# Two-direction ConvLSTM recurrences: seven packed 128-row operands in place of nine, and the state's rounding moved to ScalarE

## The reference

```python
def step(carry, xr):
    h, c = carry
    inp = jnp.concatenate([xr, h], axis=1)
    gates = lax.conv_general_dilated(inp, w_mid, (1,), 'SAME', dimension_numbers=dn) + b[None, :, None]
    i, f, g, o = jnp.split(gates, 4, axis=1)
    c2 = jax.nn.sigmoid(f) * c + jax.nn.sigmoid(i) * jnp.tanh(g)
    h2 = jax.nn.sigmoid(o) * jnp.tanh(c2)
    return ((h2, c2), h2)
```

## Time and profile before

| | us |
|---|---|
| median of 3 runs | 2088.05 |
| lowest, highest | 2082.49, 2180.3 |
| the profiled execution | 2081.32 |
| its span | 2079.5 |

### The profile page before, as it was taken

One profiled execution on the slowest core, in us unless ns is written; L12 is line 12 of the kernel. 1 busy time (PEld: TensorE's weight loads), 2 busy tenths in 40 slices (PEclk: granted clock), 3 DMA queues, 4 the chain that ended last, 5 costly groups with the idle time before them and its releaser, 6 DMA issues. The chain is left out here.

```text
span 2079.5 us, 43778 instructions
## 1 busy us (share of the span) xinstructions
PE 1838.4 (88%) x16306; PEld 1197.7 (58%) x16306; DVE 1388.5 (67%) x2550; ACT 1064.7 (51%) x1961; POOL 708.4 (34%) x583
## 2 busy tenths in 40 slices
PE   6979269999999999509999999999835999999999
PEld 5545147777777777207777777777512545555555
DVE  5538968888888888457888888888674234333434
ACT  1116147777777776346777777777561222222320
POOL 2010046666666655225666666665300000000000
PEclk9999679999999999759999999999976999999999
DMA  1769320000000000850000000000193001110100
GB/s 65 258 197 213 98 61 23 23 23 23 23 23 23 24 23 10 136 145 25 23 23 23 23 23 23 24 23 23 21 183 82 18 18 33 33 28 23 33 18 26
DMA packets 74618, 111.10 MB, mean 53 GB/s; under 512 B 11856, under 2 KB 31152, under 8 KB 74512
## 3 DMA queue, kind: packets, MB, share of 16 engines
q1 hardware_dynamic: 74512, 109.50, 20.3%
HBM read 71.71 MB, written 37.75 MB: 53 GB/s over the span
## 5 line engine op out<-in xcount | busy, mean ns | idle before, releaser
L668 PE MATMUL gates_l<-xh_l,w_hi_l 112*112 112x512 f32 x3072 | 819.5, 402 | 117.1 <-DVE keep_l L730 117.1
L668 PEld LDWEIGHTS gates_l<-xh_l,w_hi_l 112*112 112x112 f32 x3072 | 537.7, 175 | 315.4 <-issue 117.8
L644 POOL TENSOR_TENSOR xh_l<-xf_l,xh_l 48x512 fp32r<-48x512 f32 x256 | 360.1, 1407 | 281.8 <-ACT xh_l L687 281.4
L668 PE MATMUL gates_l<-xh_l,w_lo_l 112*112 112x512 f32 x1536 | 450.5, 402 | 0.0
L639 POOL TENSOR_TENSOR xh_l<-hs,xh_l 48x512 fp32r<-48x512 f32 x254 | 303.2, 1194 | 173.8 <-DVE hs L759 173.8
L668 PEld LDWEIGHTS gates_l<-xh_l,w_lo_l 112*112 112x112 f32 x1536 | 270.1, 176 | 97.9
L1174 PE MATMUL b_dw<-b_hid,b_diag 32*32 32x512 f32 x9120 | 313.1, 599 | 0.0
L699 ACT ACTIVATE gate_if_l<-gates_l 112x512 f32<-112x512 f32 x256 | 153.0, 598 | 246.9 <-PE gates_l L668 246.9
L739 DVE TENSOR_TENSOR keep_l<-gate_if_l,cell_l 48x512 f32<-48x512 f32 x256 | 175.5, 685 | 140.8 <-ACT gate_if_l L699 140.8
L1174 PEld LDWEIGHTS b_dw<-b_hid,b_diag 32*32 32x32 f32 x9120 | 185.7, 103 | 116.0 <-issue 48.3
L748 DVE TENSOR_TENSOR cell_l<-keep_l,add_l 48x256 f32<-48x256 f32 x512 | 196.7, 428 | 26.6
(11 more groups left out here) (148 smaller groups left out, 1236.4 us busy)
## 6 DMA issues: line engine op xcount, KB each, us to landing
xf_l<-rows SPq DMA_DIRECT2D x256, 96.0 KB, 2.0
hs<-rows SPq DMA_DIRECT2D x32, 384.0 KB, 10.3
rows<-hs SPq DMA_DIRECT2D x32, 384.0 KB, 5.0
xr<-in_x_rows SPq DMA_DIRECT2D x24, 256.0 KB, 2.7
xc<-in_x_cols SPq DMA_DIRECT2D x24, 256.0 KB, 3.0
mixed<-stage SPq DMA_DIRECT2D x24, 256.0 KB, 3.0
edged<-stage SPq DMA_DIRECT2D x24, 256.0 KB, 3.2
mixed_sb<-mixed SPq DMA_DIRECT2D x32, 192.0 KB, 3.7
```

What stands on the lines that cost most here:

```text
L644: pool.tensor_tensor(xh[far[d]:far[d] + C, d, s, 1, :, 1:W + 1], xf[far[d]:far[d] + C, s, :].rearrange("p (b w) -> p b w", b=B), xh[far[d] ...
L668: mm = nc.tensor.matmul(ps[d][m][0:K, :], weight[:, d, m, t, :], xh[0:K, d, s, part, :, t:t + W], start=(first and t == 0), stop=(last and ...
```

## The change

The same three products are packed in seven matmuls of 128 rows for each pair of gates, 14 in all. Three (one for each tap, weight chunks 1 to 3) take the tile HI of `xh`: the state's rounded part (times w_lo), x's remainder (times w_hi), and in the 32 rows that used to be empty the rounded part of 32 channels of x (times w_lo). Three (chunks 4 to 6) take the tile LO: the state's remainder, a *copy of the state's rounded part* on the other partitions, and the same 32 channels of x, all times w_hi. One (chunk 0) takes the tile `xc`: the last 16 channels of x in three shifts, twice (times w_hi and w_lo), and two rows of ones for the bias.

- SP: the rows that fill the gaps and `xc` come by four transfers from SBUF to SBUF for each step of each direction (`spread`), of 16 x 2 rows, 16 x 2 rows, 48 rows and 48 rows of 2112 bytes. They wait for the gates of the step that last used the slot. The x of both directions is loaded under one semaphore.
- ScalarE rounds x of both directions in one instruction of 112 rows, once for both directions, after the tanh of the cell of direction 1. Between the gates of direction d it rounds the state of the other direction in two halves (`state_hi`) and copies it (`copy_state`). The tanh of g is written back to its own accumulator.
- VectorE writes the unrounded state to `hs` in two halves and nothing else of it. The i x g product stays in the accumulator and the cell is one instruction. `cell` has one PSUM bank for both directions.
- The weights, 128 x 3136, are loaded into rows of `hs` not in use yet and split there by two casts and four masked subtractions.

The core of the diff (indentation reduced, removed lines of the loops left out since they are printed above):

```diff
-w_hi = sb("w_hi", [K, 2, 2, 3, K], F32R)
-w_lo = sb("w_lo", [K, 2, 2, 3, K], F32R)
...
+NCH = 7
+NW = 2 * NCH * 2 * K
+raw = hs[:, H // 2:H // 2 + WROWS, :].rearrange("p a n -> p (a n)")[:, 0:NW]
+w = sb("w", [P, 2, NCH, 2, K], F32R)
+mask = sb("mask", [P, 2, 2])
+xs = sb("xs", [P, 2, FLAT + 2 * LEAD], F32R)
+xh = sb("xh", [P, 2, 2, 2, FLAT], F32R)
+xc = sb("xc", [P, 2, 2, FLAT], F32R)
+gate_o = sb("gate_o", [P, 2, BW])
+keep = sb("keep", [P, BW])
...
+        def spread(d, s):
+            for a in range(2):
+                some = x_rows(s, slice(far[d] + a * GAP, far[d] + (a + 1) * GAP)).bitcast(F32)
+                sp.dma_start(xh[a * HALF + C:(a + 1) * HALF, d, s, :, :].bitcast(F32), some.unsqueeze(1).broadcast_to([GAP, 2, FLAT])
+                             ).then_inc(x_spread[d][s], 16)
+            rest = xs[far[d] + 2 * GAP:far[d] + C, s, LEAD - 1:LEAD - 1 + FLAT].bitcast(F32)
+            shifts = bass.AP(rest.tensor, rest.offset, [list(rest.ap[0]), [1, 3], [1, FLAT]])
+            for c in range(2):
+                sp.dma_start(xc[3 * GAP * c:3 * GAP * (c + 1), d, s, :].bitcast(F32), shifts).then_inc(x_spread[d][s], 16)
...
+        def step(k, more=2):
             for s in range(2):
+                done, ahead, split = (held(sp, 2 * k + (s + n)) for n in (1, 2, 3))
+                row_f, row_b = split, held(sp, k * -2 + (H - 4 - s))
+                if s < more:
+                    sp.wait_ge(x_lo[0], ahead)
+                    sp.wait_ge(x_lo[1], ahead)
+                    load(row_f, row_b, 1 - s)
+                for d in range(2):
+                    sp.wait_ge(gates[d][1], done)
+                    if d == 0:
+                        sp.wait_ge(x_hi, split)
+                    spread(d, s)
...
+                        split_lo(2 * k + (s + 2), d, s)
+                    if not last or s == 0:
+                        state_lo(2 * k + s, 2 * k + s if d == 0 else k * -2 + (H - 1 - s), d, s)
...
+                    def chunk(m, q, tile, lo, first=False, last=False):
+                        return nc.tensor.matmul(ps[d][m][0:K, :], w[:, d, q, m, :], padded(tile)[:, :, lo:lo + W],
+                                                start=first, stop=last)
+                    pe.wait_ge(x_spread[d][s], SPREAD * k + SPREAD)
+                    pe.wait_ge(sig_if[d], 2 * k + (s + 1))
+                    pe.wait_ge(sig_o[d], 2 * k + (s + 1))
+                    pe.wait_ge(cells[d], 2 * k + (s + 1))
+                    for m in range(2):
+                        chunk(m, 0, xc[:, d, s, :], 1, first=True)
+                    pe.wait_ge(x_lo[d], 2 * k + (s + 1))
+                    pe.wait_ge(h_hi[d], 2 * k + (s + 1))
+                    for m in range(2):
                         for t in range(3):
+                            chunk(m, 1 + t, xh[:, d, s, HI, :], t)
+                    pe.wait_ge(h_copy[d], 2 * k + (s + 1))
+                    pe.wait_ge(h_lo[d], 2 * k + (s + 1))
                     for m in range(2):
+                        for t in range(3):
+                            mm = chunk(m, 4 + t, xh[:, d, s, LO, :], t, last=(t == 2))
+                        mm.then_inc(gates[d][m], 1)
...
+        def state_hi(t, row, d, s):
+            n = near[d]
+            for j, part in enumerate(parts):
+                act.wait_ge(h_full[d], t * 2 + (j + 1))
+                hi = nc.scalar.activation(padded(xh[n:n + C, d, s, HI, :])[:, j * HB:(j + 1) * HB, 1:W + 1],
+                                          state(row, d)[:, part].rearrange("p (b w) -> p b w", b=HB), ACT.Copy)
+            hi.then_inc(h_hi[d], 1)
+        def copy_state(row, d, s):
+            f = far[d]
+            nc.scalar.activation(inner(xh[f:f + C, d, s, LO, :]), wide(state(row, d)), ACT.Copy).then_inc(h_copy[d], 1)
...
+                    if d == 0:
+                        earlier, row, slot = 2 * k + (s - 1), k * -2 + (H - s), s
+                        some = not (first and s == 0)
+                    else:
+                        earlier, row, slot = 2 * k + s, 2 * k + s, 1 - s
+                        some = not (last and s == 1)
+                    act.wait_ge(gates[d][0], 2 * k + (s + 1))
+                    nc.scalar.activation(gate_if[0:K, d, :], ps[d][0][0:K, :], ACT.Sigmoid).then_inc(sig_if[d], 1)
+                    if some:
+                        state_hi(earlier, row, 1 - d, slot)
+                    act.wait_ge(gates[d][1], 2 * k + (s + 1))
+                    nc.scalar.activation(ps[d][1][n:n + C, :], ps[d][1][n:n + C, :], ACT.Tanh).then_inc(tanh_g[d], 1)
+                    if some:
+                        copy_state(row, 1 - d, slot)
+                    nc.scalar.activation(gate_o[f:f + C, d, :], ps[d][1][f:f + C, :], ACT.Sigmoid).then_inc(sig_o[d], 1)
+                    act.wait_ge(cells[d], 2 * k + (s + 2))
+                    for j, part in enumerate(parts):
+                        nc.scalar.activation(tanh_c[f:f + C, j, 0:PART], cell[f:f + C, part],
+                                             ACT.Tanh).then_inc(tanhs[d], 1)
+                if s < more:
+                    split_hi(2 * k + (s + 3), 1 - s)
...
+                    dve.wait_ge(sig_if[d], 2 * k + (s + 2))
+                    dve.wait_ge(cells[d], 2 * k + (s + 1))
+                    nc.vector.tensor_tensor(keep[n:n + C, :], gate_if[f:f + C, d, :], cell[f:f + C, :],
+                                            ALU.mult).then_inc(kept[d], 1)
+                    dve.wait_ge(tanh_g[d], 2 * k + (s + 1))
+                    nc.vector.tensor_tensor(ps[d][1][n:n + C, :], gate_if[n:n + C, d, :], ps[d][1][n:n + C, :],
                                             ALU.mult).then_inc(added[d], 1)
+                    dve.wait_ge(kept[d], 2 * k + (s + 1))
+                    dve.wait_ge(added[d], 2 * k + (s + 1))
+                    nc.vector.tensor_tensor(cell[f:f + C, :], keep[n:n + C, :], ps[d][1][n:n + C, :], ALU.add
+                                            ).then_inc(cells[d], 1)
+                    dve.wait_ge(sig_o[d], 2 * k + (s + 2))
                     row = 2 * k + s if d == 0 else k * -2 + (H - 1 - s)
                     whole = hs[n:n + C, bass.ds(row, 1), :].rearrange("p a n -> p (a n)")
+                    for j, part in enumerate(parts):
+                        dve.wait_ge(tanhs[d], 4 * k + (2 * s + j + 1))
+                        nc.vector.tensor_tensor(whole[:, part], gate_o[f:f + C, d, part], tanh_c[f:f + C, j, 0:PART],
+                                                ALU.mult).then_inc(h_full[d], 1)
...
```

275 lines of the change are left out of this document (134 added, 141 removed).

## The result

| | before | after |
|---|---|---|
| median, us | 2085.27 (4 runs) | 2107.57 (4 runs) |
| the profiled execution, us | 2081.32 | 2105.0 |
| its span, us | 2079.5 | 2102.8 |

After to before is 1.0119, 95% interval 1.0092 to 1.0147: slower by 1.2%, within the 2% that I took as the bound and gave a chance of 0.10. One of the four executions before took 2180.3 us, in a slower state of the chip, and the ratio leaves it out. I had forecast 2197 us with a range of 2125 to 2255. The sign was as forecast and the size was not: 24 us in the profiled executions where I had 116.

The account below looks back on a forecast made before the run. TensorE bounds it before, ScalarE after; 127 pairs (a pair: both directions' slots of one time step) x (9.36 - 8.59) = +98, plus 18 for the layers' starts, on 2081.3: 2197 us, range 2125 to 2255.

Parts of the forecast that it names:

- The sign: Whole kernel: slower, chance 0.87; within 2% 0.10, faster 0.03.
- ScalarE takes TensorE's place as the bound: Recurrences: ScalarE's own work is 8.88 us a pair, over today's 8.59, while TensorE falls to 3.35 a slot.
- The order of the chain and the wait for the cell: Each slot: ScalarE's fixed instruction order, in which it waits 0.27 us for VectorE's cell before the tanh.
- Durations: ScalarE's instruction lengths per slot: half rounding about 0.42 us, tanh of g 0.58, summing to 3.93.
- The step that failed: ScalarE's chain in each slot: instruction durations plus handovers of 0.03 us, giving 9.36 a pair with the x rounding.
- My lower bound: Recurrence pair: halves of 0.35 and a tanh of 0.56 take 0.32 us off, to 9.04.
- rival 1: Recurrences: the cell wait hides, ScalarE packed at 8.88 us a pair; 2136 us, 2101 with 0.35 halves; chance 0.12.
- Rival 2: Recurrences: TensorE's clock falls to 1.2 GHz, making it the bound at 11.96 us a pair; 2527 us; chance 0.07.
- Rival 3: Recurrences: TensorE goes on setting the pace at 6.70 us a pair; 1859 us; chance 0.03.
- rival 4: Recurrences: a spread lands late, each microsecond past 13 costing one per pair; 2451 us at 15; chance 0.04.
- TensorE's slack: Recurrences: TensorE idle 1.3 us of each slot, first gates ready 0.5 to 1.1 us before ScalarE wants them.
- Transfers: Recurrences: four more SBUF-to-SBUF transfers per slot, 338 KB, hidden at no cost; DMA engines some 33% busy.

## Why the prediction was right or wrong

- *The sign* is no credit to the sum. Of the forecast's 116 us 98 lay in the pairs, which measured 1.3 less in each layer; that the kernel is slower at all is owed to the starts, and their 26 us had terms of another size and kind than the 18 forecast.
- *ScalarE takes TensorE's place as the bound.* Right: ScalarE 91% busy, two more matmuls a slot cost nothing, one more copy cost 66 us.
- *The order of the chain and the wait for the cell.* Right: forecast 0.27, measured 0.28 to 0.30; VectorE's pieces (0.61, 0.79, 0.73) came within 0.02.
- *Durations.* Nearly right. The group of the half roundings:

```profile
L759 ACT ACTIVATE xh_l<-hs 48x256 fp32r (+1 forms) x504 | 181.5, 407 | 6.1
```

  They are 407 ns where I had 420, and the tanh of g is 569 where I had 580. For the half the Trainium skill, page "VectorE: DVE Perf Modes", section "The TRN2 errata — SBUF-src ops pay a fixed extra latency per instruction", gave an estimate of 0.40; the measurement sides with the page, and that is worth 0.05 of the 0.78 (four halves a pair).
- *The step that failed* is the one that added durations and a handover of 0.03 for each instruction. From start to start the two halves take 0.74 and 0.63, not 0.87; the two tanh 0.55 and 0.64, not 0.72; the rounding of x 0.52, not 0.66. That is 0.76 of 0.78 us a pair, 97 us in 127 pairs. Shorter instructions are 0.07 of it (0.05 the halves); the rest is overlap. With the same chain and the measured pitches the pair is 8.58. My lower bound (halves of 0.35, 9.04 a pair) varied the length of the instructions and never their overlap, so the forecast's own span, from 2146, could not reach the result, and the range was carried down to 2125 only by half of rival 1. The trace of before did have a sign, on VectorE, which I read past: its group of cell halves,

```profile
L748 DVE TENSOR_TENSOR cell_l<-keep_l,add_l 48x256 f32<-48x256 f32 x512 | 196.7, 428 | 26.6
```

  has 428 ns each, yet two in a row took 0.77 and not 0.86.
- *Rival 1*, ScalarE packed at 8.88 (2136 us, or 2101 with halves of 0.35), is nearest in time and is not what happened: the wait stayed, and a packed ScalarE needs about 8.0 (8.58 less the two waits).
- *Rival 2*, the clock. It stayed at 1.00 with 0.46 and 0.99 us idle in each slot. Rival 3 is out by the chain, rival 4 by the landings of 3.0 and 2.4 us against 13 us of room: no matmul of the steady state waited for a transfer.
- *TensorE's slack.* Forecast 1.3 us a slot, by the same count 4.29 - 3.35 = 0.94, since the slot is shorter (the idle rows of 0.46 and 0.99 leave out the fill of the pipeline). The first gates were to be 0.5 and 1.1 us early and are 0.22 and 0.78.
- *Transfers.* Hidden as forecast, but the DMA engines are 67% busy and not 33% (29% by the 0.07 that stands in the earlier trace rows): five times the GB/s (102 against 20) took nearly ten times the share.
- *The start.* Forecast 9 a layer, measured 12.9. From the weights' issue to layer one's first sigmoid it is 30.4 us where it was 16.9 (267.17 to 284.07): 13.5 more.
  - The term for the weights, +4.9, had the wrong wait. They landed 6.3 us after their issue, where my rate gives 11.0, and VectorE did not wait for them. Its casts start 0.03 behind its own clearing of tiles both times, at 273.29 before (272.05 + 1.21) and at 275.94 now (275.43 + 0.48). The longer clearing costs 3.2; I had no term for it.
  - VectorE's split cost nothing (1.4 forecast): both casts took 1.86 together where I had 1.95 each. The cast of 1.67 that I took the rate from had a GpSimd instruction beside it; the same cast in layer two of before took 0.86. My lower figure for the split, "some 5", is not what its rate gives either: 3.9 and 2.4 are 6.3.
  - Rounding, four issues and landing took 6.3 (4.5), the issues 0.73 each and not 0.43.
  - The 11 matmuls took about 5.0 where the 15 before took 5.97 (278.10 to 284.07), 1.0 less and not 1.7. The ninth of the twelve on `xh`, which completes gates i and f, starts at 291.29 and lasts 0.63; the granted clock was still 0.50 from 291 to 292.
  - The other 5.0, from 291.92 to 296.97, belong to the third rounding, which I had left out altogether: I counted the issues that the first matmul waits for, and not what is queued behind all sixteen. With that rounding moved the first sigmoid came 5.8 sooner after the weights' issue (24.6); the 0.8 between is the clock, which was at 0.77 from 290 to 291 in that run, and the 11 matmuls took 4.25 (287.37 to 291.62).

## What to carry to other kernels

When the bound moves to an engine that issues many short instructions, price them from start to start, in rows where that engine runs them back to back, and let the lower end of the range hold their overlap; durations plus a handover gave 9% too much here. A wait inside such a chain is worth filling first (one rounding moved gave 32 us, a halved sum 35), but what an instruction covers where it stands has to be counted too: the same move cost 25 us where it had been cover. At a start, follow each queue to the last thing that the first gate stands behind, not to the first matmul, and look at what the engine that waits for a load is itself doing until then.
